# Layer norm moved into the programs of two dense feed-forward stages of a hybrid model, chunk by chunk

## The reference, cut to what matters

```python
x = x + _L0_attn_a_ref(_layernorm(x), ...)
x = x + _L0_ffn_ref(_layernorm(x), w1, b1, w2, b2)     # gelu(h @ w1 + b1) @ w2 + b2
x = x + _L0_attn_b_ref(_layernorm(x), ...)             # time and channel mix
x = x + _L0_ffn_ref(_layernorm(x), w1, b1, w2, b2)
x = x + _L1_attn_a_ref(_layernorm(x), ...)
...                                                    # experts, attention, experts
def _layernorm(x, axis=-1, eps=1e-05):                 # no gain, no bias
    m = jnp.mean(x, axis=axis, keepdims=True)
    v = jnp.var(x, axis=axis, keepdims=True)
    return (x - m) / jnp.sqrt(v + eps)
```

## Time and profile before

| what | value |
|---|---|
| time, median of 3 runs | 3193.41 us (3193.13 to 3195.82) |
| time of the profiled execution | 3191.57 us |
| its span, first to last instruction | 3188.6 us |
| PE busy | 2362.7 us, 74% |
| DVE busy | 1765.6 us, 55% |
| ACT busy | 1234.0 us, 39% |
| granted TensorE clock, mean | 0.864 of full speed |

### The profile page before, as it was taken

How to read it: one execution, slowest core, us unless ns; L and a number is a source line. 1 busy time by engine, 2 the same in 40 slices (tenths; PEclk the granted TensorE clock), 3 DMA queues, 4 the chain that set the end, 5 groups by cost and what they waited for, 6 DMA issues and landing times. The chain is left out here.

```text
span 3188.6 us, 48135 instructions
## 1 busy us (share of the span) xinstructions
PE 2362.7 (74%) x13512; PEld 1228.0 (39%) x13512; DVE 1765.6 (55%) x5580; ACT 1234.0 (39%) x1973; POOL 403.9 (13%) x452
## 2 busy tenths in 40 slices
PE   3649999999947328855999999999677382777382
PEld 1114344343325126532443434443254262554262
DVE  3756666666343896256565656666366324576223
ACT  2405455555524644443444444444323141343141
POOL 0000000000003000000000000000033553033554
PEclk9859999999968659877999999999888696888686
DMA  3272444443030000234111221121120142000144
GB/s 113 87 145 42 84 83 85 85 85 60 10 102 0 4 0 8 74 95 138 42 47 53 55 55 42 47 57 45 55 87 18 48 137 90 3 4 14 41 137 128
DMA packets 177882, 199.58 MB, mean 63 GB/s; under 512 B 36384, under 2 KB 117920, under 8 KB 177568
## 3 DMA queue, kind: packets, MB, share of 16 engines
q1 hardware_dynamic: 160000, 173.72, 21.9%
q0 software_dynamic: 9216, 19.02, 1.8%
q10 hardware_dynamic: 8448, 4.20, 0.4%
HBM read 127.09 MB, written 69.76 MB: 62 GB/s over the span
## 5 line engine op out<-in xcount | busy, mean ns | idle before, releaser
L810 ACT ACTIVATE at_probs<-at_score 128x1024 f32<-128x1024 f32 (+7 forms) x1024 | 654.6, 651 | 871.4 <-PE at_score L735 537.1
L835 DVE CUSTOM_DVE_ANT_0 at_masked<-at_mx,g_maskw 128x512 bf16<-128x512 f32 (+3 forms) x1024 | 483.2, 486 | 180.4 <-PE at_mx L701 176.2
L701 PE MATMUL at_mx<-at_K,at_Q 96*128 96x512 bf16 (+7 forms) x1536 | 466.5, 344 | 117.1 <-DVE at_mpart L835 39.4
L733 PE MATMUL at_score<-at_Q,at_K 96*128 96x512 bf16 (+7 forms) x1536 | 503.7, 332 | 27.0 <-issue 14.8
L735 PE MATMUL at_score<-at_Q,at_K 98*128 98x512 bf16 (+7 forms) x1536 | 506.7, 330 | 0.0
L831 DVE TENSOR_REDUCE at_mpart<-at_mx 128x1 f32<-128x512 f32 x512 | 353.8, 691 | 262.1 <-PE at_mx L701 242.8
L755 PE MATMUL at_outp<-at_probs,at_vop 128*32 128x512 f32 (+6 forms) x3072 | 445.5, 497 | 0.0
L701 PEld LDWEIGHTS at_mx<-at_K,at_Q 120*128 120x128 bf16 (+1 forms) x1536 | 148.2, 98 | 438.1 <-DVE at_mpart L835 197.4
L733 PEld LDWEIGHTS at_score<-at_Q,at_K 120*128 120x128 bf16 (+1 forms) x1536 | 149.7, 97 | 337.3 <-issue 181.1
L738 PE MATMUL at_score<-g_maskkq,g_identb 128*128 128x128 bf16 x1024 | 225.3, 220 | 0.0
L925 POOL MEMSET n_spread<- 16x128 f32 (+1 forms) x2 | 0.7, 355 | 1539.1 <-POOLq L536 1539.1
(11 more groups left out here) (488 smaller groups left out, 3413.7 us busy)
## 6 DMA issues: line engine op xcount, KB each, us to landing
at_Q<-q SPq DMA_DIRECT2D x192, 128.0 KB, 2.8
at_Q<-qr SPq DMA_DIRECT2D x72, 256.0 KB, 7.0
at_K<-kr SPq DMA_DIRECT2D x72, 256.0 KB, 8.6
q<-p_pieces SPq DMA_DIRECT2D x40, 384.0 KB, 3.2
at_K<-k SPq DMA_DIRECT2D x168, 64.0 KB, 2.3
buf<-g_zeros SPq DMA_DIRECT2D x32, 325.0 KB, 5.0
o<-at_osb SPq DMA_DIRECT2D x64, 128.0 KB
n_oc<-o SPq DMA_DIRECT2D x8, 1024.0 KB, 5.0
```

The costliest lines, as they stand in the source:

```text
L701: pe.matmul(bank[:, 0:hi - lo], Q0[0:R, g % 4, j, qt * P:(qt + 1) * P], K0[0:R, g % 4, j % KG, lo:hi], start=True, stop=True).then_inc(s_m ...
L733: pe.matmul(bank, K0[0:R0, g % 4, j % KG, kb * P:(kb + 1) * P], Q0[0:R0, g % 4, j, lo:hi], start=True, stop=False)
L810: act.activation(probs[:, kb % 2, j, kb * P:T], src, ACT.Exp, scale=cf.scale).then_inc(s_exp, 1)
L835: dve.tensor_tensor_reduce(masked[:, u % 2, 0:w], mx[:, u % 2, 0:w], k.maskw[:, CH - w:CH], 1.0, NEG, ALU.add, ALU.max, mpart[:, part, j, ...
```

## The change

`layernorm` is no longer called for the two stages. A new class `Norm` holds the same steps for one chunk, and `norm_ffn` puts them into the engines' programs of the feed-forward block, written out for all 8 chunks in place of the loop. On TensorE the transposes of chunk `ch` stand ahead of the first products of chunk `ch - 2` and the last products of chunk `ch - 3`. On ScalarE the root of chunk `ch + 1`, the normalising of chunk `ch`, the copy of turned chunk `ch - 1` and the gelus of chunk `ch - 2` follow one another. On VectorE the statistics of `ch + 1`, the normalising of `ch` and the two additions of chunk `ch - 4` do. The arithmetic is the same. `hT` becomes a tile of the block, and the weights are loaded when the block starts, now ahead of the norm.

```diff
-def ffn(nc, k, tag, hT, xs, w1, b1, w2, b2, beside=None):
+class Norm:
...
+    def root(self, act, ch):
+        act.wait_ge(self.s_var, ch + 1)
+        act.activation(self.std[:, ch, :], self.std[:, ch, :], ACT.Sqrt).then_inc(self.s_std, 1)
+
+    def normalise_rest(self, act, ch):
+        act.wait_ge(self.s_shift, ch + 1)
+        if ch >= 2:
+            act.wait_ge(self.s_tp, ch - 1)
+        for u in range(2, 4):
+            act.activation(self.ring[:, ch % 2, u, :], self.src[:, 4 * ch + u, :], ACT.Identity,
+                           bias=self.shift[:, ch, u:u + 1], scale=self.rstd[:, ch, u:u + 1]).then_inc(self.s_ra, 1)
...
+    def turn(self, pe, ch):
+        pe.wait_ge(self.s_rv, 2 * ch + 2)
+        pe.wait_ge(self.s_ra, 2 * ch + 2)
+        dst = self.turned(ch)
+        for u in range(4):
+            last = pe.transpose(dst[:, u * P:(u + 1) * P], self.ring[:, ch % 2, u, :], self.k.ident[:])
+        last.then_inc(self.s_tp, 1)
+
+
+def norm_ffn(nc, k, tag, xs, w1, b1, w2, b2, beside):
...
+            def first_products(ch):
+                pe.wait_ge(norm.s_ev, ch + 1)
+                for f in range(FT):
+                    if ch > 0:
+                        pe.wait_ge(s_g, FT * (ch - 1) + f + 1)
+                    pe.matmul(pre[:, f, :], w1s[:, f * P:(f + 1) * P], hT[:, ch * CH:(ch + 1) * CH],
+                              start=True, stop=True).then_inc(s_pre, 1)
...
+            for ch in range(NC + 3):
+                if ch < NC:
+                    if ch >= 2:
+                        pe.wait_ge(norm.s_ev, ch - 1)
+                    norm.turn(pe, ch)
+                if ch == 2:
+                    pe.wait_ge(s_w, 64)
+                if 2 <= ch < NC + 2:
+                    first_products(ch - 2)
+                if ch >= 3:
+                    last_products(ch - 3)
...
+            def gelus(ch):
+                if ch >= 2:
+                    act.wait_ge(s_y, ch - 1)
+                for f in range(FT):
+                    act.wait_ge(s_pre, FT * ch + f + 1)
+                    act.activation(g1[:, ch % 2, f, :], pre[:, f, :], ACT.Gelu, bias=b1s[:, f:f + 1]).then_inc(s_g, 1)
+
+            norm.root(act, 0)
+            for ch in range(NC + 2):
+                if ch + 1 < NC:
+                    norm.root(act, ch + 1)
+                if ch < NC:
+                    norm.normalise_rest(act, ch)
+                if 1 <= ch <= NC:
+                    norm.evacuate(act, ch - 1)
+                if ch == 2:
+                    act.wait_ge(s_w, 64)
+                if ch >= 2:
+                    gelus(ch - 2)
...
+            norm.statistics(dve, 0)
+            for ch in range(NC + 4):
+                if ch + 1 < NC:
+                    norm.statistics(dve, ch + 1)
+                if ch < NC:
+                    norm.normalise(dve, ch)
+                if ch >= 4:
+                    add(ch - 4)
...
-        hst, hT = normalised("l1")
-        with hst:
-            ffn(nc, k, "ffn0", hT, xs, *ffn_w, beside=lambda sp: fill_rows(sp, k, scr.back))
+        norm_ffn(nc, k, "ffn0", xs, *ffn_w, beside=lambda sp: fill_rows(sp, k, scr.back))
```

More of the change, by code:

```diff
@@ L430, in ffn @@
         c = Ctx(nc, st, tag)
+        hT = c.sb("hT", [P, N])
         w1s = c.sb("w1", [P, FT * P])
@@ L435, in ffn @@
         g1 = c.sb("g1", [P, 2, FT, CH])
-        pre = c.ps("pre", [P, 4, CH])
+        turned = c.ps("turned", [P, 2, CH])
+        pre = c.ps("pre", [P, FT, CH])
         y = c.ps("y", [P, 2, CH])
+        norm = Norm(nc, c, k, xs, linear_view(hT), lambda ch: turned[:, ch % 2, :])
         s_w, s_pre, s_g, s_y, s_b, s_x = (c.sem(n) for n in ("w", "pre", "g", "y", "bias_added", "x"))
@@ L446, in _ @@
             sp.dma_start(b2s[:], b2.rearrange("(a n) -> a n", a=1).broadcast_to([P, P])).then_inc(s_w, 16)
-            if beside:
-                beside(sp)
+            beside(sp)
         @block.tensor
         def _(pe):
-            pe.wait_ge(s_w, 64)
-            with pe.Fori(0, NC // 2) as i:
-                for g in range(2):
-                    for f in range(FT):
[L457 to L468, removed]
+            def first_products(ch):
[5 more added lines that the diff above has]
+                              start=True, stop=True).then_inc(s_pre, 1)
@@ new lines, in last_products @@
+            def last_products(ch):
+                pe.wait_ge(s_g, FT * ch + FT)
+                if ch >= 2:
+                    pe.wait_ge(s_x, ch - 1)
+                for t in range(4):
+                    for f in range(FT):
+                        last = pe.matmul(y[:, ch % 2, t * P:(t + 1) * P], g1[:, ch % 2, f, t * P:(t + 1) * P], w2s[:, f, :],
+                                         start=(f == 0), stop=(f == FT - 1))
+                last.then_inc(s_y, 1)
+            for ch in range(NC + 3):
[9 more added lines that the diff above has]
+                    last_products(ch - 3)
@@ L483, in _ @@
+            norm.root(act, 0)
[8 more added lines that the diff above has]
+                    act.wait_ge(s_w, 64)
+                if ch >= 2:
+                    gelus(ch - 2)
         @block.vector
         def _(dve):
-            dve.sem_inc(s_x, 2)
@@ L486, in _, with add @@
[L486 to L493, removed]
+            def add(ch):
+                xv = xs[:, 4 * ch:4 * ch + 4, :]
+                if ch == 0:
+                    dve.wait_ge(s_w, 64)
+                dve.wait_ge(norm.s_ra, 2 * ch + 2)
+                dve.tensor_tensor(xv, xv, b2s[:].unsqueeze(1).broadcast_to([P, 4, P]), ALU.add).then_inc(s_b, 1)
+                dve.wait_ge(s_b, ch + 1)
+                dve.wait_ge(s_y, ch + 1)
+                dve.tensor_tensor(xv, xv, y[:, ch % 2, :].rearrange("p (t n) -> p t n", t=4), ALU.add).then_inc(s_x, 1)
@@ L2729, in program @@
         recycle(nc)
-        hst, hT = normalised("l3")
-        with hst:
-            ffn(nc, k, "ffn1", hT, xs, *ffn_w, beside=lambda sp: fill_slots(sp, k, scr.bufs[1]))
+        norm_ffn(nc, k, "ffn1", xs, *ffn_w, beside=lambda sp: fill_slots(sp, k, scr.bufs[1]))
         recycle(nc)
```

42 lines of the change are left out of this document (added).

## The result

The changed kernel took 3165.26 us, the median of 4 runs (3161.14 to 3168.85), against 3193.27 of the kernel before beside it (4 runs, 3188.64 to 3195.82): a ratio of 0.9917, with an interval of 0.9905 to 0.9929. The forecast was 3176.5 with a range from 3169 to 3187.

The account below looks back on a forecast made before the run. VectorE bounds the norm, TensorE the products. Terms sum to 77.3 us a stage against 86.04 and 85.48, saving 16.9 from 3191.57 to 3174.7; 1.84 added for the median gives 3176.5 us, range 3169 to 3187.

Parts of the forecast that it names:

- To the transposes of chunk 2, as now.: Stage start, from first statistics to the transposes of chunk 2: 9.33 us, taken from the old norm's rows.
- These, at half clock: 1.11.: Chunk 2's four transposes on TensorE, ahead of the first product: 1.11 us at half clock.
- First products of chunk 0, up to the fourth gelu.: Stage start, chunk 0's first products with the clock rising on the way as now: 5.60 us.
- the 3.6 at the range's lower end: Chunk 0's first products if they find the clock up: 5.60 down to 3.6 us, part of the 3169 bound.
- The pause: TensorE, behind chunk 0's first products, waits for ScalarE before chunk 3's transposes: 3.21 us, once a stage.
- 1.7 us of clock: Behind the one pause in each stage, TensorE's clock drops to half for 3.4 us: 1.7 us lost.
- rival A: TensorE's clock holds through the pause: 1.7 us less in each stage, 3173 us; chance 15%.
- The rounds: TensorE's five steady rounds of transposes, first and last products: 7.44 us each, 37.2 us a stage.
- the two waits: TensorE waits for ScalarE at the transposes of chunks 5 and 6: 0.33 us each, twice a stage.
- Rival B: ScalarE late in each round: half a microsecond a round gives 3180 us, 1 us gives 3184; chance 12%.
- Rival C: A table switch holds ScalarE for twice its load, 2.56 us: slower by 5, 3198 us; chance 7%.
- The weights, VectorE and the end of the stage: No weight wait; VectorE needs 3.3 of 7.4 us a chunk; stage ends with 3.58, 0.19 and 0.69 us.

Follow-up runs that it names:

- e8: Kernel before with the new norm's code in a block of its own ahead of the unaltered products: 3188.41 us, ratio 0.9996.
- e7: Changed kernel with an extra gelu and root of one number a partition behind each root from chunk 4 on: 3196.59 us, ratio 1.0018.
- e5: Changed kernel with 24 unread identity transposes on TensorE in the pause ahead of chunk 3's transposes: 3164.88 us, ratio 0.9918.
- e1: Changed kernel once more, unaltered, against the kernel before: 3166.91 us, ratio 0.993, 22.7 us under the kernel before.
- e6: Changed kernel with the gelus' wait for the product put ahead of the wait for the last products: 3170.36 us, one run.
- e3: Changed kernel with TensorE's first products of a chunk ahead of the transposes of the chunk two further on: 3155.25 us, ratio 0.9892.
- e4: Kernel before with only its weight loads issued early, in the norm's block: 3182.64 us, ratio 0.9979.
- e9: Changed kernel with first products ahead of transposes, plus 16 and 4 unread identity transposes ahead of chunks 0 and 1: 3152.24 us, ratio 0.987.

## Why the prediction was wrong, point by point

The mechanism was right and the sizes were off, in two steps. The stage's sum was 1.5 and 2.9 us too long, most of it in three terms: the norm "as now", the first products, and the clock behind the second stage's pause. And the step from the sum to a median missed by another 6.7 us. The terms of the sum, in us:

| term | forecast | first stage | second stage |
|---|---|---|---|
| first statistics to the transposes of chunk 2 | 9.33 | 8.68 | 8.60 |
| these, to the first product | 1.11 | 0.88 | 0.88 |
| first product to chunk 0's fourth gelu | 5.60 | 5.02 | 5.42 |
| from there to the transposes of chunk 3 | 3.21 | 3.13 | 3.12 |
| round behind the pause, with its clock | 9.14 | 9.17 | 7.48 |
| the next four rounds | 30.42 | 30.33 | 30.32 |
| the rest, to the end of the last addition | 18.48 | 18.55 | 18.55 |
| sum | 77.3 | 75.76 | 74.37 |

- **"To the transposes of chunk 2, as now."** Mis-sized by 0.7. I read it from the old norm, but the diff writes the norm anew. e8 shows it by itself: the new one brings these transposes 0.7 us earlier in the old place too. Which part of its new form does that wasn't tried.
- **"These, at half clock: 1.11."** Mis-sized by 0.23. I took a modelled duration; the next matmul starts 0.88 us after the first transpose (930.39 to 931.27). From start to start would have been right.
- **"First products of chunk 0, up to the fourth gelu."** 5.02 and 5.42 instead of 5.60, which came from the old loop. They depend on when the clock rises: in the kernels with this order the eight products take from 4.50 (e7, second stage) to 6.11 us (e5). In the first stage, where they took 4.54, TensorE no longer set this term. The table load stands behind the wait for the product in chunk 0 too, and from 933.27 on it and the four gelus follow without a gap: 2.00 us from the first product to the load, 1.29 for the load, 1.73 to the fourth gelu. So the 3.6 at the range's lower end left out this load; with it and a full clock an estimate from the prediction's own rows is 1.06 + 1.30 + 3 x 0.59 = 4.1 us.
- **The pause** came where it was forecast and cost 3.13 and 3.12 instead of 3.21, counted from the fourth gelu's start. Its **1.7 us of clock** came in one stage and not in the other, so the forecast held for the first and rival A for the second; e1 repeated both. The ground for taking 1.7, the nearer length in the earlier trace rows, failed: the pause of 3.16 us, near the 3.27 that had lost the clock, kept it, and that of 3.61, near the 3.47 that had kept it, lost it. That one stage came out as forecast was luck.
- **The rounds.** 30.33 against 30.42, and the two waits, at the transposes of chunks 5 and 6, were there with 0.26 instead of 0.33 us; e6 removed them by moving the table load, as the order list had led me to expect.
- **Rival B** (ScalarE late every round) did not come about. e3 runs at 25.09 busy of 26.00 us without a wait.
- **Rival C** (a switch costs twice its load) did not come about, but e7 made nearly its condition: with 3.0 us more in each of the four rounds that switch twice, the kernel took 3196.59, 6 us more than the kernel before beside it, where the rival gave 5 more. The Trainium skill's rule that speaks against the change ("ScalarE: Activation LUTs", section "What ACT_TABLE_LOAD costs", 2.66 us a switch) is not what this case measures: 1.30 us from the load to what follows, in e7 three times in a row.
- **The weights, VectorE and the end of the stage** were as forecast: no wait for weights is left, and no statistics came late. The writes of zeros that now run beside the first chunks cost VectorE nothing that shows: a chunk's four statistics took 0.87 us, as before.

The stages' terms make 21.4 - 16.9 = 4.5 us of the miss of 11.2. The rest is in how the sum was set against a median. The profiled execution after took 3168.85, only 0.15 us below the range; 1.2 us are in what lies around its span (2.97 before, 1.75 after), it stands 3.6 above its own median, and I had added 1.84 for the median of three runs before, which was high: three groups of runs gave 3189.6 to 3191.2. With these the forecast's 16.9 would have been some 3173 to 3174, and the measured gap is 22.7 (e1). The **range** belongs to this second step: below, it took in a held clock and faster first products, but neither a norm that is itself quicker nor the spread between executions (7.7 us among the four of the changed kernel, up to 16 elsewhere), from which a median of three or four is not free. Its lower end lay 24.4 us under the median it was set against; the 22.7 of e1 is less than that, the first group's 28.0 more.

Where the 22.7 us come from: some 7 are the early weights (e4). The quicker norm is worth 0.7 a stage at the transposes of chunk 2 (e8). The rest, about 14, is left for the interleaving of five chunks' norms with products; that it adds up so is argued from the difference and was not run by itself. The first pair of traces divides the 21.4 us of the two stages otherwise. The first product stands 17.3 us earlier in each: 5.8 and 5.7 were the wait for weights, 0.7 the quicker norm, 10.9 the norm of five chunks. From the first product to the end the stages now take 7.1 and 6.2 us more, with transposes, pause and waits among the products. So the interleaving alone nets 3.9 and 4.7 us, 8.6 together. The two ways differ mostly by what goes with the weights: in e4 1.30 us of the wait stayed and the first products took longer. How much of the gain is the interleaving's stays open between 8.6 and 14 us.

## What to carry to other kernels

When a stage in front is woven into the one that follows, look for the one step of the pipeline's start at which the engine that bounds it has nothing else queued: here one exchange in its program order (e3) was worth as much a stage as three fifths of the whole change. A path that is written anew is not "as now": cost its instructions from the diff, and from start to start, not by the durations of modelled ends. And a forecast against a median of a few runs needs the spread of single executions in its range, however exact the sum of the stage is.

## What the runs showed of the hardware that was not expected

- The length of a pause doesn't tell alone whether TensorE's clock falls. Behind a pause of 3.61 us it stood at 0.62 and 0.88, behind one of 3.16 at 1.00 (both in the changed kernel), and behind one of 3.15 (e6, first stage) the next eight products took 6.14 us, against 3.60 at full clock. In the second stage of e7 two pauses of 3.10 us in consecutive rounds differ: behind the one the eight products took 3.60 us, behind the other 5.30. The two pauses that the prediction had to choose from the earlier trace rows had shown the same. What decides stays open.
- Work that is added only to keep TensorE busy moves the clock's rise but is no sure gain: e5 and e9 won 1.7 and 1.3 us where it hit, and the kernel's time did not show either.
- A switch of ScalarE's table is 1.30 us and no more, also three times in a row with an activation of 0.2 us between (e7).
